# One product for the last network's second half: its second and output weights multiplied for all eight experts beforehand

## The chip, the cores and the metric

The kernel runs on one core of a Trainium2 chip. The metric is the device time of one execution in microseconds (us), as the median of several runs. All arithmetic that this text is about is in float32. A float32 matmul stands in the trace as two matmul records of TensorE (PE), each with a weight load (PEld) of its own.

## The reference, cut to what matters

Four batches of 512 tokens with 256 numbers each go through an attention-like sum over a context, a network of eight experts with a router, a 16-head attention, and a last network. Only the last one is changed by its arithmetic:

```python
last = hidden_states[:, -1, :]
logits = gelu(last @ Wp1 + bp1) @ Wp2 + bp2
sel = argmax(softmax(logits), axis=-1)            # one expert of 8 for a whole batch
w1, w2 = W1[sel], W2[sel]                         # 256 x 512 and 512 x 256
h = gelu(hidden_states @ w1 + b1[sel])            # 512 tokens x 512
reasoned = h @ w2 + b2[sel]                       # 512 x 256
out = reasoned @ Wo + bo                          # 512 x 256
return hidden_states + 0.3 * out
```

Since nothing stands between them, `(h @ w2 + b2) @ Wo + bo` is `h @ (w2 @ Wo) + (b2 @ Wo + bo)`.

## The kernel before, in words

Every engine has its own written-out list of instructions, and semaphores tie the lists together. There is no planner for the stretches that matter here; for the attention a list of small pieces (FAST) sets which of them stands at which step. The program has these stages, with the spans of the profiled execution:

1. **Context and first network, 0 to 213 us.** TensorE multiplies; the transposed, normalised tokens lie in `xnT` (one block of 512 columns and two halves for each batch), the normalised tokens in `xn`. The first network's router needs them again: they are stored to DRAM, from where its tokens are gathered by expert.
2. **The router, 213 to 281 us.** VectorE works through long chains of small operations (a search in ten rounds, prefixes, masks). Beside it TensorE makes keys and values of the later attention (`last_keys`). Two times it multiplies for nothing to stay active, `keep_busy(6)` and `keep_busy(12)` (a helper that multiplies the identity with constants, 256 columns each; L945).
3. **The expert loop, 281 to 362 us.** Ten turns of a hardware loop. A turn makes two blocks of 128 tokens: hidden products (L1023), the turning of the next blocks (L1005), answers (L1031). GpSimd gathers the token rows of a later turn by an indirect DMA and scatters the answers. SyncE's queue loads the keys of the first batch beside it (`keys(0, half)`).
4. **The way on.** A value read from memory chooses between a general way and a fast way (a branch at L1440 on TensorE); the fast way is taken. TensorE there multiplies for nothing 27 times, in parts of 12, 3, 8 and 4, between waits for the gathered answers, VectorE's sums and its roots. Then ScalarE has normalised the first batch (L1512) and TensorE turns it (L1100): the attention's queries begin.
5. **The attention, 395 to 616 us**, unchanged but for the place of a bias sum on GpSimd.
6. **The last network, 617 to 701 us.** For each batch: `part4_hidden` (L1126, 8 matmuls of 512 columns), a gelu by ScalarE (L1549), `reasoned` (L1135, 8 matmuls of 512 columns: the answer transposed, in two halves), the bias and copy by VectorE (`answers`, L1958), `out` (L1145, 8 matmuls of 256 columns: times Wo), and `final` (L1966: times 0.3 plus the rows). GpSimd has before added `0.3 * bo` to the rows (L2279). Batch 3 is late, since its attention is: its projection (L1076), its normalisation on VectorE and GpSimd, its turning, its router product (L1109) and choice stand among the work of batches 0 to 2. The weights of the chosen expert are loaded by SyncE's queue as soon as the choice is known (`expert`, L796 to L800).

A SyncE instruction that waits holds all that stands behind it in that queue. TensorE's sequencer, which waits on semaphores, reads registers and branches, works ahead of the matmuls that it has handed over.

## Time and profile before

| what | value |
|---|---|
| time, median of 3 runs (lowest to highest) | 707.11 us (705.66 to 710.93) |
| the profiled execution: its own time | 703.1 us |
| the profiled execution: span of the trace | 701.3 us |
| mean clock granted to TensorE | 0.972 of full |
| TensorE busy | 633.8 us, 90% of the span |
| chain of waits: share of TensorE, VectorE, issue | 71%, 17%, 5% |

The span is the stretch in which instructions are recorded. The busy share of TensorE is high, but its records overlap, so the distance from one group's start to the next one's tells what it costs. "Idle before" in a row is the time in which the engine did nothing ahead of the group, and the releaser is what it waited for.

### The profile page before, as it was taken

How to read it: one execution, taken by the hardware profiler on the slowest of the kernel's cores; microseconds unless marked ns; L12 is line 12 of the kernel's file. 1: busy time of each engine (PE TensorE's matmuls, PEld its weight loads, DVE VectorE, ACT ScalarE, POOL GpSimd, SP SyncE). 2: the span in 40 equal slices, each digit the busy share in tenths (PEclk: the TensorE clock that was granted, in tenths of full speed). 3: DMA queues.
4: the chain of work that ended last, by engine and by line, in shares of the span. 5: the costliest groups of instructions: out<-in, count | busy, mean ns of one | idle time of the engine just before them, and what ended most of it. 6: DMA issues, size and time to landing. Idle time of an engine off the chain costs nothing.

```text
span 701.3 us, 8981 instructions
## 1 busy us (share of the span) xinstructions
PE 633.8 (90%) x3019; PEld 379.4 (54%) x3021; DVE 330.7 (47%) x1043; ACT 259.9 (37%) x353; POOL 119.0 (17%) x180
## 2 busy tenths in 40 slices
PE   3999999999998777799969789999899899999996
PEld 2666666666666445799967334334344334343643
DVE  4334233003005776232227487687877877432302
ACT  1111111111112232234421567675675675842210
POOL 0000000000002001345540160510330320403000
PEclk9999999999999799999998899999999999999999
DMA  9993302503001114512224963435515000401021
GB/s 314 361 367 102 129 0 77 180 0 123 2 1 38 45 54 144 118 60 67 75 70 124 117 93 47 66 73 103 83 38 93 2 2 2 121 26 36 31 91 60
DMA packets 48132, 61.97 MB, mean 88 GB/s; under 512 B 7959, under 2 KB 41272, under 8 KB 47688
## 3 DMA queue, kind: packets, MB, share of 16 engines
q1 hardware_dynamic: 45944, 55.66, 30.4%
q0 software_dynamic: 2144, 5.77, 2.9%
q8 instruction: 22, 0.36, 0.2%
q14 instruction: 22, 0.18, 0.1%
HBM read 43.89 MB, written 10.93 MB: 78 GB/s over the span
## 4 chain that ended last, share of the span: by engine, by line
PE 71%; DVE 17%; issue 5%; ACT 3%; DMA 2%; POOL 1%; DVEq 0%; POOLq 0%; ACTq 0%; SPq 0%
PE ps L861 13%; PE ps L872 13%; DVE arena L2102 7%; PE ps L1418 6%; PE ps L1023 4%; PE ps L1400 4%; PE ps L1135 4%; PE ps L1031 4%; PE ps L1303 3%; PE ps L1126 3%; DVE arena L1803 3%; PE ps L1145 2%; PE ps L945 2%; PE ps L1326 2%; PE ps L1051 1%
## 5 line engine op out<-in xcount | busy, mean ns | idle before, releaser
L1628 ACT ACTIVATE arena<-ps 100x1024 f32<-100x1024 f32 x128 | 124.0, 1020 | 59.4 <-PE ps L1400 59.1
L2102 DVE TENSOR_REDUCE arena<-ps 128x1 f32<-128x400 f32 x256 | 129.0, 563 | 33.6 <-PE ps L1303 32.7
L861 PE MATMUL ps<-xnT,arena 128*128 128x512 f32 x208 | 102.3, 617 | 0.9 <-DVE xnT L1688 0.9
L872 PE MATMUL ps<-arena 128*128 128x256 f32 x416 | 99.0, 382 | 0.0
L872 PEld LDWEIGHTS ps<-arena 128*128 128x128 f32 x416 | 80.1, 193 | 33.5 <-issue 25.0
L1456 ACT ACTIVATE arena<-ps 128x512 f32<-128x512 f32 x52 | 31.0, 597 | 175.3 <-PE ps L861 175.3
L1303 PE MATMUL ps<-arena 97*128 97x400 bf16 x256 | 76.1, 339 | 4.8 <-DVE arena L2102 2.3
L1400 PE MATMUL ps<-arena 100*100 100x512 bf16 x256 | 75.9, 380 | 0.1
L1418 PE MATMUL ps<-arena 100*32 100x512 f32 x512 | 68.6, 604 | 0.6 <-ACT arena L1628 0.6
L1303 PEld LDWEIGHTS ps<-arena 97*128 97x128 bf16 x256 | 20.3, 97 | 76.5 <-DVE arena L2102 48.5
L1688 DVE COPY xnT<-ps 128x512 f32<-128x512 f32 x16 | 10.4, 686 | 99.8 <-PE ps L834 99.8
L861 PEld LDWEIGHTS ps<-xnT,arena 128*128 128x128 f32 x208 | 40.0, 196 | 30.9 <-issue 28.7
L1400 PEld LDWEIGHTS ps<-arena 100*100 100x100 bf16 x256 | 31.3, 126 | 23.6 <-ACT arena L1628 6.6
L1873 DVE COPY arena<-arena 128x1024 f32 x22 | 15.3, 694 | 56.7 <-PE ps L1023 55.1
L1023 PE MATMUL ps<-arena 128*128 128x128 f32 x320 | 39.0, 282 | 1.3 <-DVE arena L1884 1.3
L1023 PEld LDWEIGHTS ps<-arena 128*128 128x128 f32 x320 | 38.8, 199 | 2.0 <-DVE arena L1884 1.5
L2219 POOL MEMSET arena<- 128x1920 f32 x2 | 3.4, 1724 | 212.7 <-PE ps L872 212.7
L1031 PE MATMUL ps<-arena 128*128 x160 | 36.2, 379 | 0.0
L1031 PEld LDWEIGHTS ps<-arena 128*128 128x128 f32 x160 | 29.6, 190 | 3.6
L1135 PE MATMUL ps<-arena 128*128 128x512 f32 x64 | 28.3, 595 | 1.6 <-ACT arena L1549 1.6
L1126 PE MATMUL ps<-xnT,arena 128*128 128x512 f32 x64 | 28.8, 598 | 0.8 <-ACT arena L1549 0.8
L945 PE MATMUL ps<-cst 128*128 128x256 f32 x90 | 23.5, 426 | 5.6 <-issue 5.6
(232 smaller groups left out, 695.8 us busy)
## 6 DMA issues: line engine op xcount, KB each, us to landing
arena<-in_W SPq DMA_DIRECT2D x16, 512.0 KB, 9.3
arena<-in_ctxT SPq DMA_DIRECT2D x4, 1664.0 KB, 7.8
arena<-in_ctxN SPq DMA_DIRECT2D x4, 1664.0 KB, 12.8
arena<-arena SPq DMA_DIRECT2D x48, 128.0 KB
arena<-in_pW SPq DMA_DIRECT2D x8, 512.0 KB, 4.4
last_k_parts<-arena SPq DMA_DIRECT2D x24, 100.0 KB, 1.8
arena<-last_k_parts SPq DMA_DIRECT2D x8, 300.0 KB
x_tok<-in_x SPq DMA_DIRECT2D x4, 512.0 KB, 9.3
```

The costliest lines, as they stand in the source:

```text
L861: ins = pe.matmul(ps[:, 4 + k % 2, :], ctxT_s[:, b % 2, c, f * P:f * P + P], xnT[:, c, S * b:S * b + S], start=(c == 0), stop=(c == KC - 1))
L872: ins = pe.matmul(ps[:, b % 2 * 2 + t // 2, t % 2 * D:t % 2 * D + D], hid[:, (k - 2) % 4, t * P:t * P + P], ctxN_s[:, b % 2, f, :], start= ...
L945: pe.matmul(ps[:, 0, 0:2 * P], eye, cst[:, 0:2 * P], start=True, stop=True, skip_group_check=True)
L1023: ins = pe.matmul(ps[:, j, f * P:f * P + P], w1_now[:, j, k, f * P:f * P + P], xsT[:, j, k, :], start=(k == 0), stop=(k == KC - 1), skip_g ...
L1031: ins = pe.matmul(ps[:, 4 + j, 0:D], hexpT[:, j, f, :], w2_s.rearrange("p e f d -> p (e f d)")[:, bass.ds(place[j] + f * D, D)], start=(f ...
L1126: ins = pe.matmul(ps[:, u % 2, :], p_w1[:, b, k, f * P:f * P + P], xnT[:, k, S * b:S * b + S], start=(k == 0), stop=(k == KC - 1))
L1135: ins = pe.matmul(ps[:, 2 + m, :], p_w2[:, b, f, m * P:m * P + P], hT[:, b % 2, f, :], start=(f == 0), stop=(f == FC - 1))
L1303: pe.matmul(o[:, 0:KF], Q2[0:KR + 1, i, g * HG + h, j * P:j * P + P], K2[0:KR + 1, i, g * HG + h, :], start=True, stop=True).then_inc(s_ma ...
L1400: ins = pe.matmul(ps[0:KT, 2 + 2 * (c % 2) + j, :], K2[0:KROWS, b % 2, h, t * KT:t * KT + KT], Q2[0:KROWS, b % 2, h, :], start=True, stop= ...
L1418: ins = pe.matmul(ps[VW * j:VW * j + VW, 6, :], V2[0:KT, bv % 2, tv, i % NG * HG + j, :], pexp2[0:KT, (c + j // 2) % 4, j % 2, :], start=( ...
L1628: act.activation(pexp2[0:KT, c % 4, :, :], ps[0:KT, 2 + 2 * (c % 2):4 + 2 * (c % 2), :], ACT.Exp).then_inc(f_pe, 1)
L2102: dve.tensor_reduce(nm2[:, m // MU % 2, h, j:j + 1], ps[:, FAST.bank(x), 0:KF], AX.X, ALU.max, negate=True).then_inc(s_by["dve"], 1)
```

## The change: what it does

**The merged weights.** For each of the eight experts TensorE multiplies W2 (given transposed, `pW2T`) with Wo: 8 matmuls of 256 columns into two PSUM banks. ScalarE copies them over the place where W2 was loaded, and SyncE's queue stores them to DRAM (`w2o_d`, 512 KB each). W2 of expert b and 4 + b lie in block b of `xnT` and of `xn`, which are free between the first network and the queries. The biases are merged by three matmuls and stored with the factor 0.3.

**Where they stand.** Merge 0 takes the place of `keep_busy(6)`; merge 1 stands behind the last keys; the bias and merges 2 and 3 take the place of `keep_busy(12)` ahead of the expert loop; merges 4 to 7 stand behind the loop, ahead of the branch. In the fast way 14 idle products are left of 27. Merges 0 to 3 are stored during the loop, each when a later pair of token blocks has landed; the keys of batch 0 are loaded at the first two such points. Merges 4 to 7 are stored behind the loads of the gathered answers.

**The last part.** `reasoned` and `answers` are gone. `out` multiplies `hT` with the merged weights, 16 matmuls of 256 columns per batch, and waits for each gelu by itself; that of batch 3 is in two halves, each with its sum and its store. GpSimd adds the loaded, merged bias per batch (`biases`). The pieces of batch 3 (turning, router) stand elsewhere among the rest.

```diff
+            def load_second_weights(b):                       # SyncE
+                sp.wait_ge(s_w2l, 16 * (3 + 2 * b))
+                sp.wait_ge(s_tpf, 2 * KC + KC * 2 + MASK_TURNS + (KC + 1) * (b + 1))
+                sp.wait_ge(s_xnst, 16 * ((b if b < 2 else B - 1) + 2))
+                for e in (b, B + b):
+                    sp.dma_start(second_weights(e), a["pW2T"][e].rearrange("(h p) n -> p h n", p=P)).then_inc(s_w2l, 16)
...
             sp.wait_ge(s_ekst[0], 48 * KC * B // 2)
-            sp.wait_ge(s_xsb, 64)
             for half in range(2):
+                sp.wait_ge(s_xsb, 32 * (3 + half))
                 keys(0, half)
             key_ones(0)
+            for n in range(MERGED_EARLY):
+                sp.wait_ge(s_xsb, 32 * (5 + n))
+                store_merged(n)
...
+            sp.wait_ge(s_w2s, 16 * (MERGED_EARLY + 1))        # behind the loads of the answers
+            for n in range(MERGED_EARLY, E):
+                store_merged(n)
...
+            def merge_weights(n, bank):                       # TensorE
+                if n % 2 == 0:
+                    pe.wait_ge(s_w2l, 16 * (3 + 2 * (n // 2 + 1)))
+                w = second_weights(MERGED[n])
+                for f in range(FC):
+                    for k in range(KC):
+                        ins = pe.matmul(ps[:, bank + f // 2, f % 2 * D:f % 2 * D + D], w[:, k, f * P:f * P + P], wof[:, k, :],
+                                        start=(k == 0), stop=(k == KC - 1), skip_group_check=True)
+                ins.then_inc(s_w2p, 1)
...
-            keep_busy(12)
+            for k in range(KC):
+                pe.matmul(ps[0:E, 0, 0:D], pb2t[:, k, :], wof[:, k, :], start=(k == 0), stop=False, skip_group_check=True)
+            pe.matmul(ps[0:E, 0, 0:D], cst[0:1, C_ONES:C_ONES + E], bo_s[:, :], start=False, stop=True, skip_group_check=True).then_inc(s_w2p, 1)
+            merge_weights(2, 2)
+            pe.wait_ge(s_w2c, merged(1))
+            merge_weights(3, 4)
...
             block_transposes()
+            pe.wait_ge(s_w2c, merged(MERGED_EARLY - 1))
             with pe.Fori(0, pairs) as i:
...
+            merge_weights(4, 2)
             pe.wait_ge(s_xsT, pairs * 2 + 2)
             pe.wait_ge(s_expd, 1)
+            merge_weights(5, 4)
+            pe.wait_ge(s_w2c, merged(4))
+            merge_weights(6, 2)
+            pe.wait_ge(s_w2c, merged(5))
+            merge_weights(7, 4)
...
-            def out(b):
-                pe.wait_ge(s_rtc, KC * (b + 1))
+            def out(b, parts=1):
                 if b >= 2:
                     pe.wait_ge(s_fo, b - 1)
-                for t in range(TB):
-                    for k in range(KC):
-                        ins = pe.matmul(ps[:, 4 + 2 * (b % 2) + t // 2, t % 2 * D:t % 2 * D + D], rT[:, b % 2, k, t * P:t * P + P], wof[:, k, :],
-                                        start=(k == 0), stop=(k == KC - 1))
-                ins.then_inc(s_po, 1)
+                n = TB // parts
+                for part in range(parts):
+                    for f in range(FC):
+                        pe.wait_ge(s_p4a, b * FC + f + 1)
+                        for t in range(part * n, part * n + n):
+                            ins = pe.matmul(ps[:, 4 + 2 * (b % 2) + t // 2, t % 2 * D:t % 2 * D + D], hT[:, b % 2, f, t * P:t * P + P],
+                                            p_w2[:, b, f, :], start=(f == 0 and t % 2 == 0), stop=(f == FC - 1), skip_group_check=True)
+                    ins.then_inc(s_po, 1)
...
-                keep_busy(12)
                 pe.wait_ge(s_gat[0], 16)
-                keep_busy(3)
+                keep_busy(2)
                 pe.wait_ge(s_moe, 1)
                 keep_busy(8)
...
+            def take_merged(n, bank):                         # ScalarE
+                act.wait_ge(s_w2p, merged(n))
+                for h in range(KC):
+                    ins = act.activation(second_weights(MERGED[n])[:, h, :], ps[:, bank + h, :], ACT.Copy)
+                ins.then_inc(s_w2c, 1)
...
                 act.wait_ge(s_lnst, roots or B * k + b + 1)   # norm(b, k)
+                act.wait_ge(s_w2s, 16 * (E + 1) if b else 16 * (MERGED_EARLY + 1))
```

TensorE's list around the end of the expert loop, before: L1031 are the answers, L1015 and L1035 belong to the loop's end and a register, L1440 is the branch (what stands directly behind it is the general way).

```order
L1031 MATMUL ps<-arena 128x256
L1015 REGISTER_ALU
L1015 COMPARE_AND_BRANCH
L1035 ISA
L1440 COMPARE_AND_BRANCH
L834 MATMUL ps<-cst,xn 128x128 x8
```

The same place in the changed kernel; L1097 are the answers, L1001 the merges, L1495 the branch.

```order
L1097 MATMUL ps<-arena 128x256
L1081 REGISTER_ALU
L1081 COMPARE_AND_BRANCH
L1001 MATMUL ps<-wof,xnT 128x256 x8
L1102 ISA
L1001 MATMUL ps<-wof,xn 128x256 x8
L1001 MATMUL ps<-wof,xnT 128x256 x8
L1001 MATMUL ps<-wof,xn 128x256 x8
L1495 COMPARE_AND_BRANCH
```

Four merges of 8 matmuls now stand between the loop and the branch.

TensorE's list of the last part, before: L1076 is batch 3's projection, L1126 hidden, L1135 reasoned, L1145 out, L1100 batch 3's turning.

```order
L1076 MATMUL ps<-wo,xnT 128x256 x8
L1135 MATMUL ps<-arena 128x512 x8
L1126 MATMUL ps<-xnT,arena 128x512 x8
L1135 MATMUL ps<-arena 128x512 x8
L1100 MATMUL ps<-cst,xn 128x128 x8
L1145 MATMUL ps<-arena 128x256 x8
L1109 MATMUL ps<-xnT,arena 128x1 x2
L1145 MATMUL ps<-arena 128x256 x8
L1117 MATMUL ps<-arena 1x8
L1126 MATMUL ps<-xnT,arena 128x512 x8
L1135 MATMUL ps<-arena 128x512 x8
```

And in the changed kernel: L1150 is the projection, L1200 hidden, L1212 out, L1174 the turning, L1183 and L1191 the router.

```order
L1150 MATMUL ps<-wo,xnT 128x256 x8
L1212 MATMUL ps<-arena 128x256 x16
L1200 MATMUL ps<-xnT,arena 128x512 x2
L1174 MATMUL ps<-cst,xn 128x128 x8
L1200 MATMUL ps<-xnT,arena 128x512 x4
L1183 MATMUL ps<-xnT,arena 128x1 x2
L1200 MATMUL ps<-xnT,arena 128x512 x2
L1191 MATMUL ps<-arena 1x8
L1212 MATMUL ps<-arena 128x256 x16
L1200 MATMUL ps<-xnT,arena 128x512 x8
L1212 MATMUL ps<-arena 128x256 x16
```

The groups of L1135 are gone, each out has 16 matmuls instead of 8, and batch 3's turning and router product stand within the hidden products of batch 1.

## Rows read from the trace of the kernel before

**Rows 1.** Page, part 1: each engine's busy us, share of the span, instructions.
```profile
PE 633.8 (90%) x3019; PEld 379.4 (54%) x3021; DVE 330.7 (47%) x1043; ACT 259.9 (37%) x353; POOL 119.0 (17%) x180
```

**Rows 2.** Timeline of TensorE's tail: start us, us, instructions [idle before <-releaser].
```profile
627.63 7.03 PE L1135 MATMUL ps<-arena 128*128 128x512 f32 x16
634.50 3.60 PE L1126 MATMUL ps<-xnT,arena 128*128 128x512 f32 x8
638.49 3.70 PE L1126 MATMUL ps<-xnT,arena 128*128 128x512 f32 x8 [0.40 <-ACT arena L1549]
642.97 7.13 PE L1135 MATMUL ps<-arena 128*128 128x512 f32 x16 [0.78 <-ACT arena L1549]
...
655.13 3.73 PE L1145 MATMUL ps<-arena 128*128 128x256 f32 x16 [0.35 <-ACT arena L1535]
...
663.05 3.70 PE L1126 MATMUL ps<-xnT,arena 128*128 128x512 f32 x8 [0.44 <-ACT arena L1549]
667.53 7.13 PE L1135 MATMUL ps<-arena 128*128 128x512 f32 x16 [0.78 <-ACT arena L1549]
...
681.37 3.62 PE L1145 MATMUL ps<-arena 128*128 128x256 f32 x16
684.83 7.03 PE L1135 MATMUL ps<-arena 128*128 128x512 f32 x16
692.78 3.73 PE L1145 MATMUL ps<-arena 128*128 128x256 f32 x16 [0.92 <-DVE arena L1958]
```

**Rows 3.** Timelines of ScalarE and then VectorE, same stretch.
```profile
636.46 1.28 ACT L1549 ACT_TABLE_LOAD   x1 [10.19 <-PE ps L1126]
637.75 1.26 ACT L1549 ACTIVATE arena<-ps,arena 128x512 f32<-128x512 f32 x2
...
696.61 1.29 DVE L1966 SCALAR_TENSOR_TENSOR x_tok<-ps,x_tok 128x512 f32<-128x512 f32 x2 [3.89 <-PE ps L1145]
```

**Rows 4.** Timeline of TensorE ahead of the expert loop.
```profile
272.43 0.37 PE L997 MATMUL ps<-arena 128*128 128x56 bf16 x8 [3.46 <-DVE arena L1856]
...
273.85 6.72 PE L945 MATMUL ps<-cst 128*128 128x256 f32 x24
281.49 0.63 PE L1005 MATMUL ps<-cst,arena 128*128 128x128 f32 x4 [0.92 <-DMA arena<-xn_rows,token_of_slot]
283.43 5.38 PE L1023 MATMUL ps<-arena 128*128 128x128 f32 x32 [1.31 <-DVE arena L1884]
```

**Rows 5.** TensorE's sequencer, by line: duration ns, first and last start us.
```profile
L1009 PEldq TENSOR_LOAD <-lst_i x1: 769/769/769, 276.5 to 276.5; - x1
...
L1015 PEldq MOVE  x1: 33/33/33, 281.5 to 281.5; - x1
...
L1019 PEldq EVENT_SEMAPHORE  x10: 51/51/51, 283.3 to 353.4; - x10
...
L1440 PEldq COMPARE_BRANCH  x1: 4917/4917/4917, 362.7 to 362.7; - x1
```

**Rows 6.** Timeline of TensorE behind the expert loop.
```profile
367.68 14.07 PE L945 MATMUL ps<-cst 128*128 128x256 f32 x54 [5.58 <-issue]
381.58 0.60 PE L1100 MATMUL ps<-cst,xn 128*128 128x128 f32 x4
```

**Rows 7.** Timeline of ScalarE behind the expert loop.
```profile
378.05 2.07 ACT L1512 ACTIVATE xn<-x_tok,minus_mean_by_root,rstd 128x256 f32<-128x256 f32 x4 [15.53 <-DVE minus_mean_by_root L1677]
```

**Rows 8.** Chain of waits in the expert loop: start us, us, what.
```profile
292.74 4.87 DMA arena<-xn_rows,tokens_to_load
...
354.00 3.94 DMA arena<-xn_rows,tokens_to_load
```

**Rows 9.** Stretches: length, busy us of each engine, TensorE's granted clock, DMA.
```profile
283.30:286.70 3.40, 3.27 (x15) 3.30 (x16) 0.00 (x0) 0.00 (x0) 1.56 (x3) 0.50 0.27 77
...
365.20:372.00 6.80, 4.32 (x10) 3.48 (x11) 0.00 (x0) 0.00 (x0) 0.18 (x1) 0.50 0.54 171
```

**Rows 10.** DMA issues: KB each, median us from issue to landing.
```profile
xn_rows<-xn SPq DMA_DIRECT2D x4, 512.0 KB, 5.5
```

More of the change, by code:

```diff
@@ L602, in _, with store_merged @@
             store_tokens(3)
+            for b in range(2, B):
+                load_second_weights(b)
+            def store_merged(n):
+                e = MERGED[n]
+                sp.wait_ge(s_w2c, merged(n))
+                sp.dma_start(w2o_d[e].rearrange("p (h n) -> p h n", n=S), second_weights(e)).then_inc(s_w2s, 16)
             def store_keys(b):
@@ L807, in _ @@
                     expert(b, b - lo, i)
-            for b in range(B):
+            for b in range(B - 1):
                 sp.wait_ge(s_fo, b + 1)
@@ L811, in _ @@
                              x_tok[:, TB * b:TB * b + TB, :]).then_inc(s_out, 16)
-            sp.wait_ge(s_out, 16 * B)
+            for j in range(2):
+                lo = TB * (B - 1) + 2 * j
+                sp.wait_ge(s_fo, B + j)
+                sp.dma_start(a["out"][lo * P:(lo + 2) * P, :].rearrange("(t p) d -> p t d", p=P), x_tok[:, lo:lo + 2, :]).then_inc(s_out, 16)
+            sp.wait_ge(s_out, 16 * (B + 1))
         @block.tensor
@@ L951, in _ @@
             pe.wait_ge(s_res, 4)
-            keep_busy(6)
+            merge_weights(0, 0)
             for b in range(3, 4):
@@ L1160, in last_part @@
                 route(pieces, 2)
-                taken(pieces, ("route", 2))
+                part4_hidden(1, 3, FC)
+                route_logits(pieces, 2)
                 out(1)
-                pe.wait_ge(s_fo, 1)
-                route_logits(pieces, 2)
                 part4_hidden(2, 0, FC)
-                for m in range(KC):
-                    reasoned(2, m)
+                out(2)
                 part4_hidden(3, 0, FC)
-                taken(pieces, ("logits", 2))
-                out(2)
-                for m in range(KC):
-                    reasoned(3, m)
-                out(3)
+                out(3, 2)
             tp_before = tp[0]
@@ L1286, in general_way @@
                 part4_hidden(0, 0, FC)
-                for m in range(KC):
-                    reasoned(0, m)
                 last_part(GENERAL)
@@ L1488, in _ @@
                 last_keys(c)
+            take_merged(1, 4)
+            act.wait_ge(s_w2p, MERGED_BIAS)
+            act.activation(bo2[:, :], ps[0:E, 0, 0:D], ACT.Copy, scale=0.3).then_inc(s_w2c, 1)
+            for n, bank in ((2, 2), (3, 4)):
+                take_merged(n, bank)
             act.wait_ge(s_slot, 1)
@@ L1502, in _ @@
             act.sem_inc(s_expd, 1)
+            for n, bank in ((4, 2), (5, 4), (6, 2), (7, 4)):
+                take_merged(n, bank)
             act.wait_ge(s_list, 1)
@@ L1974, in last_part @@
             def last_part(pieces):
-                for m in range(KC):
-                    answers(1, m)
+                final(0)
                 for k in range(KC):
                     take_turned(pieces, ("last turn4", B - 1, k))
-                final(0)
-                final(1)
                 route_shift(pieces, 2)
                 choose(2)
-                for m in range(KC):
-                    answers(2, m)
-                final(2)
-                for m in range(KC):
-                    answers(3, m)
-                final(3)
+                for b in range(1, B):
+                    final(b)
             def general_way():
@@ L2086, in general_way @@
                     choose(i)
-                for m in range(KC):
-                    answers(0, m)
                 last_part(GENERAL)
@@ L2273, in base, with biases @@
                 pool.wait_ge(s_ln, 3 * B + b + 1)
-                if b == 0 and lo == 0:
-                    pool.wait_ge(s_w4, 16 * 6)
-                    steps.step(pool, pool.tensor_scalar(bo_s[:, :], bo_s[:, :], 0.3, None, ALU.mult))
                 rows = slice(TB * b + lo, TB * b + hi)
                 steps.step(pool, pool.tensor_tensor(x_tok[:, rows, :], x_tok[:, rows, :], xn[:, rows, :], ALU.add))
-                ins = pool.tensor_tensor(x_tok[:, rows, :], x_tok[:, rows, :], bo_s.unsqueeze(1).broadcast_to([P, hi - lo, D]), ALU.add)
-                if hi == TB:
-                    ins.then_inc(s_base, 1)
-                else:
-                    steps.step(pool, ins)
+            def biases(which):
+                for b in which:
+                    pool.wait_ge(s_pw[b], 16 * 4)
+                    rows = slice(TB * b, TB * b + TB)
+                    pool.tensor_tensor(x_tok[:, rows, :], x_tok[:, rows, :], p_bias[:, b, :].unsqueeze(1).broadcast_to([P, TB, D]),
+                                       ALU.add).then_inc(s_base, 1)
             def general_way():
@@ L2291, in general_way @@
                     base(b, 0, TB, steps)
+                biases(range(B))
             def fast_way():
```

113 lines of the change are left out of this document (61 added, 52 removed).

## The prediction

> **What bounds the kernel now.** First the page: TensorE is busy 90% of the span [rows 1], so the change must be judged by what it takes off TensorE's path and what it puts on it. Then the timeline of TensorE's tail [rows 2]: from 627.63 us, where `reasoned(0)` starts, the groups follow each other to the last `out` at 692.78 us, and the final sum starts at 696.61 us [rows 3]: 68.98 us. Read starts, not durations. A group of 16 records of 512 columns costs 6.87 us (634.50 - 627.63), one of 256 columns 3.46 us (684.83 - 681.37). In that stretch stand four `reasoned` and three hidden groups (7 x 6.87 = 48.1 us), four `out` (13.8 us), and 1.5 us of turning and router products, which I estimate from what is left between neighbouring groups. These make 63.4 us, so 5.6 us are gaps, and the rows with brackets show where. Last the two places where the merges go: ahead of the loop [rows 4] and behind it [rows 6], and what the sequencer does there [rows 5].
>
> **The tail.** *Matmuls.* Four `reasoned` and four `out` go: 4 x (6.87 + 3.46) = 41.3 us. Four `out` of 32 records come: 4 x 2 x 3.46 = 27.7 us. On the path in full, since TensorE is the path: **-13.6 us**.
>
> *Gaps.* By starts, the gap ahead of 638.49 us is 0.56 us (8 records cost 3.43), of 642.97 us 1.05, of 655.13 us 0.41, of 663.05 us 0.70, of 667.53 us 1.05, of 692.78 us 1.08 [rows 2]. Those of 1.05 us are `reasoned` waiting for the last gelu (0.69 us, [rows 3]); the new `out` asks for its last hidden part only after 24 of its 32 records, 5.2 us in, so the gelu is hidden. That of 692.78 us is VectorE's `answers`, which is gone. Those of 638.49 and 663.05 us come from a table load of 1.28 us in front of two gelus [rows 3]; in batch 1 the turning of batch 3 now stands behind the first hidden part and covers it, in batch 2 it stays. That of 655.13 us waits for the router's gelu; a hidden part now stands in its place. So all but 0.70 us go: **-4.1 us**.
>
> *The end.* The last sum is two operations of 0.65 us [rows 3]; only the second one is now behind the last product: **-0.65 us**. The last store is half as large; I take nothing for it, since its latency stays.
>
> What could be late next: the weights of batch 3. Its choice is made some 15 us earlier, as batch 3's router stands earlier, and hidden(3) starts 10 us earlier; the distance grows. GpSimd's `biases` for batches 0 and 1 stand ahead of batch 3's `norm`, about 4 us of sums, but fall into the 15 us in which GpSimd would wait for VectorE's roots. Nothing for both. Tail: **-18.4 us**.
>
> **Ahead of the loop.** Merge 0 has 16 records for the 12 of `keep_busy(6)` and ends before batch 3's normalised tokens come: nothing, and its two copies are done before the router's exponential: nothing; if that cover were gone, 0.7 us. Merge 1 (3.46 us) falls into the gap of 3.46 us that ends at 272.43 us [rows 4]: +0.2 us at most, and VectorE's second half of the marks, at 273.47 us, hides it. From 273.85 us come the bias (6 records of 256 columns, 1.3 us) and merges 2 and 3 (6.9 us): they end at 282.1 us. Now the new wait: the loop is entered only when ScalarE has copied merge 3, two copies of at most 0.69 us each [rows 3], so at 283.4 us. Queued behind this wait on the sequencer is its own register work for a turn, from L1015's move at 281.5 us to L1019's wait at 283.3 us, 1.8 us [rows 5]. The first hidden product then starts at 285.2 instead of 283.43 us [rows 4]: **+1.8 us**. Before, the clock granted in the 3.40 us from 283.30 us was 0.50 [rows 9], the 1.2 GHz level, after TensorE had idled for most of 280.6 to 283.4 us; the 32 records took 5.2 us instead of 3.6. The idle now is 2.6 us: I take the same low level again; if it stays high, -1.6 us.
>
> **In the loop.** A turn hangs on the gathered rows about as much as on TensorE: the landing took 3.94 us in one turn and 4.87 us in the second, when the keys' loads ran beside it [rows 8]. These move to later turns: -0.9 us. Four stores of 512 KB come in, each started when a pair has landed; such a store took 5.5 us to land [rows 10], and next gathers are issued some 3 us after its start. Bounds: 0, or 5.5 us each. I take +0.2 us each, near the lower bound, since the turn with keys beside it lost only 0.9 us. Sum 0. The new loads of the second weights delay the first keys' stores by some 7 us in SyncE's queue; the buffers are needed again 15 us later: nothing.
>
> **Behind the loop.** TensorE's last answers end at 361.9 us. Before, the sequencer waited for the last copies and then spent 4.92 us in the branch, from 362.7 us [rows 5]; the idle products began at 367.68 us and ended at 381.58 us [rows 6], though ScalarE had finished at 380.12 us [rows 7] what the turning waits for. So TensorE is late there already, and the merges push it. Four merges: 4 x 3.46 = 13.8 us, to 375.8 us. The sequencer works ahead: it read L1009's register at 276.5 us [rows 5] while the 24 records issued before it ran until 280.6 us [rows 4]. Merge 7 waits for the copies of merge 5 (370.2 us), and its instructions are handed over in some 2 us, so the branch runs from 372.3 to 377.3 us, under merge 7 but for 1.5 us. Then come 14 idle products, 28 records, 6.0 us: 383.4 us against 381.58: **+1.8 us**. The clock should stay high over 1.5 us of idleness; before it fell in a gap of 5.6 us (0.50 from 365.20 us, [rows 9]). ScalarE copies merge 7 by 377.2 us and is due at 378.05 us [rows 7]: nothing. Stores 4 to 7 stand behind the gathered answers in the same queue; the wait of batch 1's normalisation for them ends near 384 us and it is due at 391 us: nothing.
>
> The Trainium skill (Runtime: NRT & Kernel Launch, Instruction fetch mechanics) says that a taken branch to a target outside the window of two fetched pages stops the engine until the page has been fetched by DMA. The branch of 4.92 us agrees. It speaks against work placed ahead of a branch: where the window happened to hold the target, the sum would be 1.5 us lower; where nothing overlaps, it is the first rival below.
>
> **Sum.** -18.4 + 1.8 + 0 + 1.8 = **-14.8 us**, from the profiled execution's 703.1 us to 688.3 us. The median of the runs is 4.0 us above that execution; the same distance gives 707.1 - 14.8 = 692.3, rounded **692 us**.
>
> **Rivals.**
> *The branch does not overlap.* It starts when merge 7 is done: 375.8 + 4.9 + 0.1 = 380.8 us, then 6.0 us of idle products and 2 us for the low clock at their start, as before (54 records took 14.07 us and not 11.7, [rows 6]): 388.9 us, +7.3 instead of +1.8 us. 697.8 us. For it: the branch did wait for everything before. Against it: L1009. Chance 0.14.
> *The stores cost more in the loop.* At 2 to 3.5 us per store, the gain falls by 8 to 14 us: 700 to 706 us. Chance 0.09.
> *Slower.* Each store of 512 KB stands in full before the gathered rows of the next turn: 4 x 5.5 = 22 us, net +7.2: 714 us. It decides from 3.7 us per store on. For it: turns at 354.00 us already waited on a landing. Against it: the store starts as early in the turn as it can. Chance 0.04.
> *More gain.* The clock stays high at the loop's start (-1.6), the branch's target is at hand (-1.5), the small store lands earlier: 688 us. Chance 0.09.
> The forecast, 689 to 696 us: 0.64.
>
> **Range.** 685 to 700 us: it holds the forecast, the first and the last rival, and the bounds of small terms (the tail between -13.6, if all gaps come back, and -19); it leaves out the second and third, 0.13. About 1%, 7 us, is what a measurement can tell from no change. Faster by more: forecast, first and last rival and a bit of the second, 0.88. Within: 0.08. Slower: 0.04.
>
> **What would show it.** Tail: 16 records of 256 columns every 3.46 us, no gap between hidden and out, a stretch of some 50.6 us in place of 68.98. Loop start: first hidden product 1.8 us after the copies of merge 3. Branch: first idle product 1.5 us behind merge 7, the turning 7.6 us behind it. Loop: ten turns in the time of before. Wrong would be: a wait of `out` on loaded weights, of batch 1's normalisation on the stores, or turns longer by more than 1 us.

## The result and the profile after

The changed kernel took 700.15 us as the median of 4 runs (698.84 to 701.76), beside 706.87 us for the kernel before on the same chip (705.66 to 710.93). The ratio is 0.9888, with a 95% interval of 0.986 to 0.9915 (not quite the quotient of the two medians, 0.9905). So the kernel is faster, clear of noise, but by 6.7 us and not by 14.8. The median lies 0.15 us above the upper end of the predicted range; by the ratio, from the 707.1 us that the forecast started from, it would be 699.2 us, just inside. Two more series with the same two kernels gave 0.9916 (0.9888 to 0.9944) and 0.9887 (0.9856 to 0.9919).

Page, part 1, of the changed kernel: each engine's busy us, share and instructions, against [rows 1].

```profile
span 697.6 us, 9158 instructions
PE 634.7 (91%) x3091; PEld 389.6 (56%) x3093; DVE 325.5 (47%) x1035; ACT 268.8 (39%) x370; POOL 120.8 (17%) x176
```

TensorE is as busy as before, in a span 3.7 us shorter. That says nothing about where the time went; the stretches between marks on TensorE's path do. The three columns on the left are the profiled executions behind the result above, the three on the right those of the last series (experiments 9 to 12). "Tail" runs from the end of batch 3's projection to the start of VectorE's last sum.

```
us                               before  changed   diff | before  changed   diff
first hidden product of the loop 283.43   284.70   +1.3 | 285.40   284.69   -0.7
the loop, ten turns               78.51    85.67   +7.2 |  78.37    76.25   -2.1
end of the loop to batch 0's turn 19.65    25.77   +6.1 |  19.00    25.34   +6.3
that to the end of projection(3) 246.05   247.48   +1.4 | 245.85   247.57   +1.7
tail                              69.59    50.73  -18.9 |  69.59    50.73  -18.9
rest                               4.03     3.26   -0.8 |   4.05     3.28   -0.8
span                             701.26   697.61   -3.7 | 702.26   687.86  -14.4
```

So the tail gave what the prediction said, and between 283 and 400 us much of it was given back. Most of what is missing in the first profile is in the loop (+7.2 us, forecast 0), then behind it (+6.1, forecast +1.8), then in the attention (+1.4, forecast nothing). The two profiled executions of the changed kernel differ in one line, the loop. A third profile of it, from the series of experiments 5 to 8, has 83.1 us for the loop, 28.5 for the stretch behind it, 248.9 for the one up to projection(3) and the same tail. In that one the clock was granted at 0.50 once more at 432 us, which the other two don't have. So the stretches with waits in them vary from one execution to the next.

**The tail.** Timeline of TensorE, changed kernel, against [rows 2]: start us, us, instructions, what it waited for.

```profile
643.62 7.07 PE L1212 MATMUL ps<-arena 128*128 128x256 f32 x32
650.52 1.88 PE L1200 MATMUL ps<-xnT,arena 128*128 128x512 f32 x4
652.24 1.04 PE L1174 MATMUL ps<-cst,xn 128*128 128x128 f32 x8
...
658.93 7.17 PE L1212 MATMUL ps<-arena 128*128 128x256 f32 x32
665.94 3.60 PE L1200 MATMUL ps<-xnT,arena 128*128 128x512 f32 x8
669.92 3.70 PE L1200 MATMUL ps<-xnT,arena 128*128 128x512 f32 x8 [0.39 <-ACT arena L1619]
673.46 7.07 PE L1212 MATMUL ps<-arena 128*128 128x256 f32 x32
680.37 7.03 PE L1200 MATMUL ps<-xnT,arena 128*128 128x512 f32 x16
687.24 7.07 PE L1212 MATMUL ps<-arena 128*128 128x256 f32 x32
```

Read the starts: an `out` of 32 records costs 6.91 us (673.46 to 680.37), a hidden group of 16 records 6.87 us. One gap with a releaser is left, the table load in batch 2 that the prediction left standing. VectorE, the last sum, against [rows 3]:

```profile
694.34 0.69 DVE L2030 SCALAR_TENSOR_TENSOR x_tok<-ps,x_tok 128x512 f32<-128x512 f32 x1 [2.69 <-PE ps L1212]
```

**Ahead of the loop.** TensorE, against [rows 4].

```profile
274.50 3.72 PE L1001 MATMUL ps<-wof,xnT 128*128 128x256 f32 x16
278.05 3.62 PE L1001 MATMUL ps<-wof,xn 128*128 128x256 f32 x16
281.51 0.60 PE L1070 MATMUL ps<-cst,arena 128*128 128x128 f32 x4
284.70 5.44 PE L1089 MATMUL ps<-arena 128*128 128x128 f32 x32 [2.59 <-issue]
```

**Behind the loop.** TensorE, then ScalarE, against [rows 6, 7].

```profile
370.37 3.62 PE L1001 MATMUL ps<-wof,xnT 128*128 128x256 f32 x16
...
380.73 3.62 PE L1001 MATMUL ps<-wof,xn 128*128 128x256 f32 x16
387.86 3.13 PE L993 MATMUL ps<-cst 128*128 128x256 f32 x8 [3.52 <-issue]
391.70 4.59 PE L993 MATMUL ps<-cst 128*128 128x256 f32 x20 [0.71 <-issue]
396.13 0.60 PE L1174 MATMUL ps<-cst,xn 128*128 128x128 f32 x4
```

```profile
384.38 1.09 ACT L1539 ACTIVATE xn<-ps 128x512 f32<-128x512 f32 x2 [2.37 <-PE ps L1001]
391.79 2.07 ACT L1582 ACTIVATE xn<-x_tok,minus_mean_by_root,rstd 128x256 f32<-128x256 f32 x4 [6.32 <-DMA merged_weights<-xn]
```

TensorE's branch, its sequencer by line (ns, first and last start us), against [rows 5], and the stretch of the idle products, against [rows 9]:

```profile
L1495 PEldq COMPARE_BRANCH  x1: 7488/7488/7488, 380.3 to 380.3; - x1
```

```profile
388.00:396.10 8.10, 7.39 (x28) 6.07 (x29) 7.93 (x34) 2.07 (x4) 0.00 (x0) 0.79 0.22 82
```

The four merges take the 13.8 us that were forecast. Then come 3.7 us until the first idle product, not 1.5, and 8.3 us for 28 records, not 6.0: part of them ran at the 1.2 GHz level (0.50 granted over 3.4 us), and there is a second gap among them. In the profile beside experiments 5 to 8 the same 28 records took 11.1 us, at 0.58 granted.

**The loop.** In the first profile of the changed kernel the turns took 8.1 to 8.9 us from the second on. ScalarE in one of them, behind it TensorE at the same place:

```profile
311.20 0.66 ACT L1567 ACTIVATE arena<-ps 128x256 f32<-128x256 f32 x2 [3.47 <-DMA answers_by_token<-arena,tokens_to_store]
311.88 1.28 ACT L1563 ACT_TABLE_LOAD   x1
313.17 0.60 ACT L1563 ACTIVATE arena<-ps 128x512 f32<-128x512 f32 x1
315.85 0.60 ACT L1563 ACTIVATE arena<-ps 128x512 f32<-128x512 f32 x1 [2.08 <-PE ps L1089]
```

```profile
310.66 3.81 PE L1089 MATMUL ps<-arena 128*128 128x128 f32 x32 [0.80 <-issue]
314.30 0.60 PE L1070 MATMUL ps<-cst,arena 128*128 128x128 f32 x4
```

The last hidden product starts at 314.19 us (0.11 us ahead of the turning), and ScalarE's second gelu, which waits for it alone, starts 1.66 us later. In the kernel before this distance is 0.3 us in every turn. I call this a late signal: the semaphore update that tells the other engines that the products are done comes late. TensorE itself did not stop, since the answers behind it are done in time; only its signal for the hidden products, and the two for the turned blocks, come late and within 0.1 us of each other. VectorE's copy of weights waits for the same signal, and behind it stand the next list of tokens, the gather, and TensorE's next turn. The first row's wait of 3.47 us for the scattered answers looks like the culprit. Here are ScalarE's waits for them in the whole loop (us in total, times, longest), first in this execution, then in the later one of the same kernel, whose loop took 76.3 us:

```profile
ACT arena L1567 <- DMA answers_by_token<-arena,tokens_to_store: 10.7, 7, 3.5
```

```profile
ACT arena L1567 <- DMA answers_by_token<-arena,tokens_to_store: 10.7, 4, 3.6
```

The sum is the same, so this wait is not what the 9.4 us between the two loops are made of (1.6 us of them are the first turn, at the low clock in one and not in the other).

When the late signals begin says more. TensorE and then ScalarE in turn 2 of the slow execution, and the first store of merged weights on SyncE's queue:

```profile
293.86 3.73 PE L1089 MATMUL ps<-arena 128*128 128x128 f32 x32
```

```profile
298.66 0.60 ACT L1563 ACTIVATE arena<-ps 128x512 f32<-128x512 f32 x1 [2.22 <-PE ps L1089]
```

```profile
314.04 0.67 SPq L639 DMA_DIRECT2D merged_weights<-xnT  x1
```

The last hidden product of turn 2 starts at 297.3 us and is signalled 1.3 us later, that of turn 3 at 305.5 us and 1.6 us later. The first store in the loop is issued at 314.0 us. It is the same in every profile that has late signals: those of turns 2 and 3 come before the first store, which is issued between 313.7 and 314.9 us. So the stores in the loop did not start them.

### The profile page after: what moved, and what is told of

Its sections match the earlier page's. It is cut to its first block, busy times and chain, and to the rows that moved or that the text cites. A ratio compares the mean times of both kernels' runs of the same rounds, so it can differ in the third digit from the quotient of the medians.

```text
span 697.6 us, 9158 instructions
## 1 busy us (share of the span) xinstructions
PE 634.7 (91%) x3091; PEld 389.6 (56%) x3093; DVE 325.5 (47%) x1035; ACT 268.8 (39%) x370; POOL 120.8 (17%) x176
## 4 chain that ended last, share of the span: by engine, by line
PE 70%; DVE 16%; issue 6%; DMA 3%; ACT 2%; POOL 2%; DVEq 0%; POOLq 0%; ACTq 0%; SPq 0%
PE ps L909 14%; PE ps L920 13%; DVE arena L2158 7%; PE ps L1475 6%; PE ps L1089 4%; PE ps L1457 4%; PE ps L1001 4%; PE ps L1200 4%; PE ps L1361 3%; PE ps L1212 3%; PE ps L1097 3%; DVE arena L1874 3%; PE ps L1384 2%; PE ps L1125 1%; PE ps L987 1%
## 5 line engine op out<-in xcount | busy, mean ns | idle before, releaser
L920 PE MATMUL ps<-arena 128*128 128x256 f32 x416 | 99.0, 382 | 0.0
L1361 PEld LDWEIGHTS ps<-arena 97*128 97x128 bf16 x256 | 20.4, 97 | 78.2 <-DVE arena L2158 50.1
L909 PEld LDWEIGHTS ps<-xnT,arena 128*128 128x128 f32 x208 | 39.8, 195 | 30.7 <-issue 28.5
L1097 PE MATMUL ps<-arena 128*128 x160 | 37.4, 382 | 0.1
L1097 PEld LDWEIGHTS ps<-arena 128*128 128x128 f32 x160 | 29.2, 190 | 5.3 <-issue 1.9
L1200 PE MATMUL ps<-xnT,arena 128*128 128x512 f32 x64 | 28.9, 596 | 0.4 <-ACT arena L1619 0.4
L1212 PE MATMUL ps<-arena 128*128 128x256 f32 x128 | 28.4, 380 | 0.0
L2276 POOL DMA_INDIRECT arena<-xn_rows,tokens_to_load x20 | 19.5, 973 | 41.1 <-DVE tokens_to_load L1962 38.1
```

Source lines behind the costliest of these rows:

```text
L909: ins = pe.matmul(ps[:, 4 + k % 2, :], ctxT_s[:, b % 2, c, f * P:f * P + P], xnT[:, c, S * b:S * b + S], start=(c == 0), stop=(c == KC - 1))
L920: ins = pe.matmul(ps[:, b % 2 * 2 + t // 2, t % 2 * D:t % 2 * D + D], hid[:, (k - 2) % 4, t * P:t * P + P], ctxN_s[:, b % 2, f, :], start= ...
L1097: ins = pe.matmul(ps[:, 4 + j, 0:D], hexpT[:, j, f, :], w2_s.rearrange("p e f d -> p (e f d)")[:, bass.ds(place[j] + f * D, D)], start=(f ...
L1200: ins = pe.matmul(ps[:, u % 2, :], p_w1[:, b, k, f * P:f * P + P], xnT[:, k, S * b:S * b + S], start=(k == 0), stop=(k == KC - 1))
L1212: ins = pe.matmul(ps[:, 4 + 2 * (b % 2) + t // 2, t % 2 * D:t % 2 * D + D], hT[:, b % 2, f, t * P:t * P + P], p_w2[:, b, f, :], start=(f = ...
L1361: pe.matmul(o[:, 0:KF], Q2[0:KR + 1, i, g * HG + h, j * P:j * P + P], K2[0:KR + 1, i, g * HG + h, :], start=True, stop=True).then_inc(s_ma ...
```

## The experiments

Three series, each with the kernel before beside it on one chip (experiments 1 to 4, 5 to 8, and 9 to 12). All have the new last part; its tail was 50.73 us in every one of them.

**1. The tail alone.** Edit (the merges, their copies and stores and the loads of second weights are left out, so the last part multiplies with other numbers):

```diff
-            merge_weights(0, 0)
+            keep_busy(6)
...
-            merge_weights(2, 2)
-            pe.wait_ge(s_w2c, merged(1))
-            merge_weights(3, 4)
+            keep_busy(12)
...
-            merge_weights(4, 2)
```

> The new last part alone: the merges, their copies, their stores and the loads of the second weights are left out, the idle products stand as before the change, and the last part loads W2 transposed and the plain bias in the place of the merged ones. By the sum of the prediction the tail is worth 18.4 us: the whole 688.5 to 689 us against 707 us of the kernel before. The profile of the changed kernel shows 19.7 us for this stretch: 687 us. If a part of the gain of the tail is lost in the attention (1.4 us longer in the changed kernel) even without the merges: 688.5 us. The loop 78.5 us, the turning of the first batch at 381.6 us as before the change.

Measured: 683.27 us (682.37 to 685.39) beside 703.7; ratio 0.971 (0.9693 to 0.9726), 20.4 us faster. From the end of the loop to the turning 19.9 us, the attention 246.0 us, as before the change. So the tail's 18.4 us is shown, with 1 to 2 us on top, and all that is missing belongs to the merges with their copies, loads and stores. The changed kernel itself was not run in this series; the three kernels with the merges that were (experiments 2 to 4) took 9.5 to 10.9 us more than this one. One forecast was missed: the loop took 80.5 us and not 78.5, since its second turn, with the early keys beside it, took 12.7 us where the later ones took 7.5.

**2. to 4. What slows the loop.** Edits: without the four stores in the loop (the last part then loads other numbers of the same size); with the early keys; both.

```diff
-            for n in range(MERGED_EARLY):
-                sp.wait_ge(s_xsb, 32 * (5 + n))
-                store_merged(n)
```

```diff
+            sp.wait_ge(s_xsb, 64)
             for half in range(2):
-                sp.wait_ge(s_xsb, 32 * (3 + half))
                 keys(0, half)
```

> The changed kernel without the four stores of merged weights during the expert loop (the last part then loads W2 transposed in the place of the merged weights, the same number of bytes). The loop, from the first hidden product to merge 4, took 85.7 us in the changed kernel and 78.5 us before. Theory A (the stores delay the landing of the scattered answers, on which ScalarE's copies wait): 79 to 80 us, and the whole 5 to 6 us faster than the changed kernel, about 694 us. Theory B (the keys of the first batch, loaded in turns 2 and 3 instead of turn 1, push the loop out of step, and it stays so): 83 to 85 us, the whole 699 us. Theory C (neither; TensorE's signals come late for a reason of its own, since the last three turns have no transfer of SyncE and are slow too): 84 to 86 us, 700 us.

Measured: 693.12 us, ratio 0.9858 (0.984 to 0.9877); the loop 75.5 us.

> The changed kernel with the keys of the first batch loaded both at once when the first four blocks have landed, as before the change; the four stores stay. Theory A (stores): turns 1 to 3 as before the change, the loop 84 to 85 us, the whole within 1 us of the changed kernel, 700 us. Theory B (keys): the loop back to 79 to 80 us, the whole about 694 us. Theory C: 84 to 86 us, 700 us.

Measured: 692.81 us, ratio 0.9846 (0.9821 to 0.9871); the loop 78.2 us, with all four stores in it.

> Both of the two edits before together: in the loop SyncE's queue then does what it did before the change. Theories A and B: 78.5 to 79 us for the loop, the whole about 693.5 us. Theory C: 84 us or more, 700 us, and then the cause is in the program outside of SyncE's queue.

Measured: 694.12 us, ratio 0.9872 (0.9853 to 0.9892); the loop 77.6 us.

No theory had this: each single edit brought the loop back, and no profile of the series had a late signal, the one with the stores included. Either the edits or the chip had to be behind it, so the changed kernel itself was run again.

**5. The changed kernel again, with other edits beside it.**

> The changed kernel once more, for a second profile beside the other kernels of this series. Theory D (in the changed kernel the second hidden products of a turn signal 1.0 to 1.8 us late, from turn 2 on to the end of the loop, because the late keys and the stores together brought the loop out of step): the loop 84 to 87 us again, the ratio to the kernel before 0.987 to 0.990. Theory E (this lateness belongs to that one execution and not to the program): the loop 76 to 79 us, the ratio 0.980 to 0.985, less than that of the kernel with early keys (0.9846).

Measured: 700.92 us beside 706.17, ratio 0.9916 (0.9888 to 0.9944). The loop 83.1 us, signals up to 1.5 us later than usual. Theory D's numbers, but its cause is wrong: the late signals are there before the first store, and the next three have them with other moments of the stores and of the keys.

**6. Stores at another moment.**

```diff
-                sp.wait_ge(s_xsb, 32 * (5 + n))
+                sp.wait_ge(s_ys, 32 * (3 + n) + 16)
```

> The changed kernel (late keys) with the four stores started when the answers of turns 3 to 6 have been scattered, and no longer when the next blocks are gathered. Theory D, with the stores beside the scatter as what brings the loop out of step: the loop 76 to 78 us. If it is the late keys: 84 to 87 us as in the changed kernel. Theory E: 76 to 78 us, as the changed kernel itself in this series.

Measured: 700.38 us, ratio 0.9935 (0.991 to 0.996), the loop 81.7 us with late signals. The first store was issued 6.0 us into turn 4 instead of 3.4 us, and the signals of turns 2 and 3 were late again ahead of it. Their moment is not it. Nor are the late keys: the kernels of 7 and 8 load the keys early, as that of experiment 3 did, and in this series both have late signals and loops of 83.0 and 83.6 us.

**7. Without the idle products** (on the kernel with early keys):

```diff
-                pe.wait_ge(s_gat[0], 16)
-                keep_busy(2)
-                pe.wait_ge(s_moe, 1)
-                keep_busy(8)
-                pe.wait_ge(s_lnst, 2 * 0 + 1)
-                keep_busy(4)
```

> The kernel with early keys without its 14 idle products behind the branch. With them the turning starts at 391.0 us, though ScalarE has finished the normalisation at 387.4 us. If the idle products only delay: from the end of the loop to the turning 23.6 us instead of 27.15, the whole 3.5 us faster, 689.5 us. If the clock, at half rate behind the branch, stays low for the queries without them: the turning 3.5 us earlier and the first query products 2 to 3 us later behind it, the whole 0 to 1.5 us faster.

Measured: 697.09 us, ratio 0.9872 (0.9838 to 0.9906). From the end of the loop to the turning 22.9 us. TensorE, then ScalarE, of this kernel:

```profile
379.55 3.62 PE L1001 MATMUL ps<-wof,xn 128*128 128x256 f32 x16
392.10 1.09 PE L1174 MATMUL ps<-cst,xn 128*128 128x128 f32 x4 [8.93 <-ACT xn L1576]
393.96 1.09 PE L1174 MATMUL ps<-cst,xn 128*128 128x128 f32 x4 [0.78 <-ACT xnT L1654]
395.78 5.47 PE L1125 MATMUL ps<-xnT,wq 128*128 128x512 f32 x8 [0.73 <-ACT xnT L1654]
```

```profile
383.20 1.08 ACT L1533 ACTIVATE xn<-ps 128x512 f32<-128x512 f32 x2 [2.37 <-PE ps L1001]
389.88 2.07 ACT L1576 ACTIVATE xn<-x_tok,minus_mean_by_root,rstd 128x256 f32<-128x256 f32 x4 [5.59 <-DMA merged_weights<-xn]
```

Now the turning waits for ScalarE's normalisation, and that did not wait for its input: VectorE's roots were ready at 384.4 us, the copy of merge 7 at 384.3. The 5.6 us between are ScalarE's own register loads and its own branch, which stand in its list behind the copies. Before the change they lay in the 15.5 us in which it waited for the roots [rows 7]. The idle products are worth something too: without them the eight query records behind the turning took 5.5 instead of 3.7 us, at the 1.2 GHz level (0.50 granted). The stretch from the turning to the end of projection(3) took 248.9 us. That is no more than in the changed kernel of this series (248.9), but 1.8 more than in the kernel with early keys of experiment 3 (247.1, another chip), so only the 1.8 us of the query records can be put down to the missing products.

**8. The merges behind the branch** (early keys, no idle product):

```diff
-            merge_weights(4, 2)
...
             def fast_way():
+                take_merged(4, 2)
+                take_merged(5, 4)
                 norm(0, 0, 1)
+                take_merged(6, 2)
+                take_merged(7, 4)
...
-                pe.wait_ge(s_gat[0], 16)
-                keep_busy(2)
...
-                keep_busy(4)
+                late_merges()
```

> The kernel with early keys, and merges 4 to 7 moved behind the branch, in the place of all 14 idle products; ScalarE takes them there too, the normalisation of the first batch standing between the second and the third. From the end of the loop to the turning of the first batch: 27.2 us with the merges ahead of the branch, 19.65 us in the kernel before. Theory F (the branch costs its 3.2 us behind merge 7 and a further 2 us for the code behind it, ScalarE's own branch holds the normalisation back, and idle products follow): 5.7 us of branch as before, 13.8 us of merges and 2.4 us for the low clock, 22 us, 5 us less, the whole 688 us. Theory G (the branch costs the same wherever it stands, only hidden or not; the merges are the whole price): 25 to 27 us, 692 us.

Measured: 691.83 us (691.38 to 692.42), ratio 0.9801 (0.9774 to 0.9828); 9.1 us below the changed kernel of the same series. TensorE behind the loop, its branch, and ScalarE:

```profile
372.97 6.15 PE L1001 MATMUL ps<-wof,xnT 128*128 128x256 f32 x16 [4.92 <-issue]
378.96 3.62 PE L1001 MATMUL ps<-wof,xn 128*128 128x256 f32 x16
...
385.87 3.62 PE L1001 MATMUL ps<-wof,xn 128*128 128x256 f32 x16
389.32 0.60 PE L1176 MATMUL ps<-cst,xn 128*128 128x128 f32 x4
```

```profile
L1493 PEldq COMPARE_BRANCH  x1: 4257/4257/4257, 368.7 to 368.7; - x1
```

```profile
382.61 1.08 ACT L1537 ACTIVATE xn<-ps 128x512 f32<-128x512 f32 x2 [2.37 <-PE ps L1001]
383.97 2.08 ACT L1578 ACTIVATE xn<-x_tok,minus_mean_by_root,rstd 128x256 f32<-128x256 f32 x4 [0.27 <-DVE minus_mean_by_root L1750]
```

21.4 us from loop to turning, against 28.5 us for the changed kernel in this series: theory F, with 22 forecast. This edit does two things, and experiment 7 tells them apart. Dropping the 14 idle products alone took the stretch from 28.5 to 22.9 us; moving the merges behind the branch took it from there to 21.4, and the attention from 248.9 to 246.9, with the first query records at the full clock again (3.7 us). By the medians, 3.8 us of the 9.1 are the first step and 5.3 the second. The normalisation starts 0.27 us behind the roots again, and no gap is left between the merges.

**9. to 12. Both kernels once more, without the stores, and the best version.**

> The kernel before once more, for a profile beside the next three on the same chip. The changed kernel's late signals of TensorE (1.0 to 1.8 us behind the last hidden product, from turn 2 on) showed in both profiles of it, and in those of all kernels with stores in the loop but one, which ran on another chip. Theory H (they come from the stores in the loop): no late signal here, the loop 78.5 us. Theory I (they depend on the chip alone): late signals here too, if the changed kernel has them in this series; the loop then 83 us or more. The time within 0.3% of the kernel before.

Measured: 702.94 us, ratio 1.0006; the loop 78.4 us, no late signal.

> The changed kernel for the third time, as the measure for this series. Late signals and a loop of 83 to 86 us, as twice before: ratio 0.988 to 0.992. If they depend on the chip, none and a loop of 75 to 78 us: ratio 0.978 to 0.982.

Measured: 694.42 us, ratio 0.9887 (0.9856 to 0.9919). The profiled run took 689.78 us, with a loop of 76.3 us and no late signal, with every store in it. The other three took 693.2 to 695.8 us; what they did otherwise no profile shows.

> The changed kernel without the four stores in the loop, again, beside the changed kernel on the same chip. Theory H: no late signal, the loop 75.5 to 76.5 us, 7 to 9 us faster than the changed kernel. Theory I, and theory C of the first series: late signals with a loop of 82 us or more, wherever the changed kernel has them.

Measured: 693.67 us, ratio 0.9865 (0.9838 to 0.9893), the loop 77.6 us (its first turn, 9.2 us, at the low clock). Beside the changed kernel it gains 0.7 us, within the uncertainty. This run can't decide on theory H, for no kernel of this series had late signals; what speaks against H is that in the other series they begin ahead of the first store. Where they are missing, the four stores cost about 0.3 us together: the turns with a store took up to 7.63 us instead of 7.46.

The last kernel's edit on SyncE's queue (its other lines move the merges as in experiment 8, and change the banks of merges 2 and 3):

```diff
+            store_merged(0)
             for b in range(2, B):
                 store_values(b)
+            store_merged(1)
...
-            for n in range(MERGED_EARLY):
-                sp.wait_ge(s_xsb, 32 * (5 + n))
-                store_merged(n)
...
-            for n in range(MERGED_EARLY, E):
+            for n in range(2, E):
                 store_merged(n)
```

> A complete kernel from what was found: merges 4 to 7 behind the branch as in the kernel that took 21.4 us from the end of the loop to the turning; merges 0 and 1 stored before the loop, 2 and 3 behind it with 4 to 7; keys of the first batch in turns 2 and 3; merge 3 in banks that the loop doesn't use, so that the loop is entered without waiting for its copies. Theory H: the loop 75.5 us, its start at 283.5 us instead of 284.9, then 21.5 to 22 us to the turning, and the tail as it is: end at 283.5 + 75.5 + 22 + 247 + 50.7 + 3.3 = 682 us by the trace, 684 us in time, a ratio of 0.968 to 0.972. Theory I, in a series with late signals: 7 us more, a ratio of 0.979. If six stores behind the loop (3 MB instead of 2 MB) hold back the normalisation of the second batch: the attention 2 to 3 us longer.

Measured: 688.95 us (688.58 to 689.11), ratio 0.9804 (0.9778 to 0.983): the best complete version, 5.5 us below the changed kernel, yet 5 us above what was expected. Its loop took 77.7 us and started 2.2 us later than in the changed kernel:

```profile
278.12 3.62 PE L1000 MATMUL ps<-wof,xn 128*128 128x256 f32 x16
284.92 0.99 PE L1069 MATMUL ps<-cst,arena 128*128 128x128 f32 x4 [3.19 <-DMA arena<-xn_rows,token_of_slot]
286.86 6.20 PE L1088 MATMUL ps<-arena 128*128 128x128 f32 x32 [0.94 <-DVE arena L1957]
```

The store of merge 1, now issued at 273.9 us, runs beside the first gathers (issued at 274.5 and 276.0 us); TensorE waits 3.19 us for their landing and starts the loop at the low clock (its first turn took 9.9 us). They landed 9.0 us after the second was issued; in the kernel before it was 4.6 us. That the store is the cause is read from this one profile; no kernel was run to try it. The six stores behind the loop held nothing back: the stretch from the turning to the end of projection(3) took 246.6 us, the shortest with merges.

## Why the prediction was right and wrong

- **Tail, -18.4 us.** Right, in mechanism and within 0.5 us: -18.9 in the profiles. The 0.8 us behind the last sum were not forecast ("I take nothing for it"); 20.4 us by experiment 1. The products cost what was worked out, and of the gaps one is left, as said.
- **Ahead of the loop, +1.8 us.** Right in kind: the wait for merge 3's copies and the register work behind it on the sequencer show as 2.59 us of issue, and the first hidden product started at 284.7 to 284.9 us in all three profiles of the changed kernel, where 285.2 was forecast. The low clock came later in the turn in two of them (0.50 from 286.2 us); in the third it did not come, and the turn took 7.5 instead of 9.2 us, the 1.6 us that the prediction named.
- **In the loop, 0.** In the two series without late signals (experiments 1 to 4 and 9 to 12) the terms were small and of the forecast sign: the four stores cost some 0.3 us together, where 0.8 was taken, and never held the gather for 5.5 us. The keys' move was worth more than 0.9: with early keys turn 2 took 8.2 to 12.7 us in the five profiles without late signals, with late keys 7.46 us in every one. What the prediction lacked is the late signals, its largest miss: +7.2 us in the first profile, and a loop of 83.1 us in the second. They showed in all five profiles of kernels with stores in the loop there, and in no other, but two kernels with the same stores had none in the quieter series, and all five had them in turns 2 and 3, before the first store of the loop was issued. So the stores in the loop are ruled out as what starts them, and so are the late keys, by experiments 7 and 8. Whether something else in the change, ahead of turn 2, is a condition stays open, since the only profile of the kernel before in those series has none; so does the cause. In those series the kernel before, too, was 3 us slower (706 to 707 against 703 us), which its one profile there (703.1 us) does not explain. That may be why the ratios of the three series are so alike; no run shows it.
- **Behind the loop, +1.8 us: this step failed**, in every profile of the changed kernel (+6.1 and +6.3; beside experiments 5 to 8 it was 28.5 us, where the kernel before had 19.7 and 19.0). "The branch runs from 372.3 to 377.3 us, under merge 7 but for 1.5 us" was wrong: the sequencer did reach the branch 4 us ahead of merge 7's end, as argued from L1009, but then 3.3 to 3.7 us passed between that end (merge 4's start and 13.8 us) and the first idle product. The branch took 7.07 to 7.49 us and not 4.92. The trace's records of the instruction queue show where: the block of code of 16 KB that was moved during the branch started 4.7 to 5.2 us after the branch did, 0.9 to 1.3 us behind merge 7's end; before the change it started 2.6 us after the branch. In all fourteen profiles the branch ends 2.3 to 2.4 us after this block starts, however long it took before. The Trainium skill (Runtime: NRT & Kernel Launch, Instruction fetch mechanics) says that code is fetched in blocks of 16 KiB and that a taken branch out of the fetched window forces such a fetch before execution can go on; the traces agree. That the fetch waits for the matmuls ahead of it is inferred from the times; of the nine profiles with merges ahead of the branch none was otherwise (the block followed 0.6 to 1.3 us behind merge 7). So the merges ahead of the branch hid 1.3 to 1.7 us of it in the three profiles of the changed kernel, and 3.4 were counted.
- **The idle products, 6.0 us**, took 8.3, 8.3 and 11.1 us: a second block of code, moved at 389.4 us, made a gap of 0.7 us that ended 2.3 us after the block's start, and behind the 3.7 us of idleness after merge 7 the granted clock fell to 0.50, though it "should stay high" (over 1.5 us, as the prediction had it). "14 idle products" were costed, but not that nothing covers them when TensorE is late: ScalarE was done at 393.9 us, they ended at 396.1.
- **ScalarE "is due at 378.05 us: nothing"** overlooked its own branch. The prediction followed TensorE's branch and not the same one on ScalarE, which had lain under a wait; with four copies ahead of it, 5.8 to 7.0 us of register loads and branch came between the last copy and the normalisation in the three profiles. Experiment 7 shows it as the next bound, 2.2 us behind the idle products.
- **The attention, not mentioned**: +1.4 us at the first score product, which waits 1.32 us for the query rows. SyncE issued the twelve copies in 9.18 us (8.05 before), one of them in 1.76; a code block of 16 KB was moved from 406.6 us, 0.4 us ahead of that one. The kernels with the merges behind the branch have neither the block there nor the long copy, and 246.9 and 246.6 us for this stretch. That the block is the cause was not tried.
- **Rivals.** The first, the branch not overlapped, forecast +7.3 us behind the loop and 697.8 us; it is the nearest to what happened there, at +6.1 and +6.3, though half of its mechanism was wrong: the branch did not start when merge 7 was done, its fetch did. That its 697.8 us is near the measured 700.15 is in part luck, since the loop's 7.2 us are not in it. The second and third, the stores, fell where they could be tried. The measured gain, 6.7 us, is at the edge of the 7 us that the prediction called no change and gave 0.08.

## What to carry to other kernels

A branch on every engine is a cost to place, not only the one on the engine that bounds: list what each engine has ahead of its own. Where filler work (the idle products) stands behind a branch, put real work in its place instead of ahead of the branch: here the merges ahead of it were paid in full, with most of the branch and the filler on top. Work moved into a wait must be costed with what that wait covered on the other engines too. A single profile of a loop that is tied to transfers on both sides shows one phase of it; take a second one in another series before a cause is sought in the code.

## What was not expected of the hardware

- TensorE's signals came 0.6 to 2.1 us behind the start of their matmul, where 0.3 us is usual, without the matmuls behind being later, two or three bunched within 0.1 us, turn after turn, in one series and not in the next with the same program.
- The taken branch on TensorE kept the next matmul 3.0 to 3.7 us behind the end of the last one in the eight profiles that have merges ahead of it and idle products behind it, though the sequencer reached it 4 us early; from a standstill it took 4.3 to 5.1 us in five.
- With a store of 512 KB issued 0.6 us ahead of the first gathers TensorE waited 3.2 us for them (one profile, cause not tried); four of the same within the loop cost about 0.3 us together where the signals were in time.
